# Two-layer decoder on one core: the experts' down product as three fp32r products, its weights split ahead of the loop

## What is computed

```python
xn = _layernorm(x, ln_gamma, ln_beta); xf = xn.reshape(-1, D)
logits = jnp.clip(xf @ router_w.T, -CLAMP, CLAMP)
probs = jnp.clip(softmax(logits), ROUTER_EPS, 1.0)
topk_p, topk_i = jax.lax.top_k(probs, 2)
dense_gate = zeros(N, 8).at[tokens, topk_i].add(topk_p)
for eid in range(8):
    xe = xf * dense_gate[:, eid:eid + 1]
    gate, up = jnp.split(xe @ gate_up_w[eid].T, 2, axis=-1)
    hidden = jax.nn.silu(gate) * up
    out = out + hidden @ down_w[eid].T
return x + out
```

## Time and profile before

| what | value |
|---|---|
| median of 3 runs | 1375.52 us (1372.28 to 1378.48) |
| the profiled execution's own time | 1373.03 us |
| its span | 1371.3 us |
| TensorE busy (PE) | 1188.6 us, 87% |
| VectorE (DVE) | 863.6 us, 63% |
| ScalarE (ACT) | 763.2 us, 56% |
| GpSimd (POOL) | 584.4 us, 43% |
| mean granted clock of TensorE | 0.939 |
| L2388 down matmuls, x312 records | 73.9 us, 380 ns mean |
| L2567 low parts of weights, x78 | 92.1 us, 1222 ns mean |
| L2427 high parts of weights, x78 | 77.9 us, 1047 ns mean |
| L2296 scatters, x39 | 86.2 us, 2211 ns mean |

### The profile page before, as it was taken

One profiled execution on the slowest core, in us unless ns is written; L12 is line 12 of the kernel. 1 busy time (PEld: TensorE's weight loads), 2 busy tenths in 40 slices (PEclk: granted clock), 3 DMA queues, 4 the chain that ended last, 5 costly groups with the idle time before them and its releaser, 6 DMA issues. The chain is left out here.

```text
span 1371.3 us, 24976 instructions
## 1 busy us (share of the span) xinstructions
PE 1188.6 (87%) x8059; PEld 867.2 (63%) x8060; DVE 863.6 (63%) x1528; ACT 763.2 (56%) x2082; POOL 584.4 (43%) x616
## 2 busy tenths in 40 slices
PE   7888589566999999999999999999898439999992
PEld 4544367445666767677666777766676337777781
DVE  2588799874345555665355555675687766777773
ACT  2598457434556565565555655664365245565653
POOL 1155447656436332321563321200267405666663
PEclk9999779888799999999999999999999658999996
DMA  9100000001010010000100000100720232322325
GB/s 302 40 1 1 0 1 2 1 16 31 17 32 16 16 32 17 1 16 17 32 16 17 16 17 6 43 1 1 287 83 1 74 126 40 50 50 47 52 42 138
DMA packets 42136, 58.27 MB, mean 42 GB/s; under 512 B 6608, under 2 KB 34640, under 8 KB 42032
## 3 DMA queue, kind: packets, MB, share of 16 engines
q1 hardware_dynamic: 34544, 46.70, 11.3%
q0 software_dynamic: 7488, 10.23, 4.6%
HBM read 32.80 MB, written 13.63 MB: 34 GB/s over the span
## 5 line engine op out<-in xcount | busy, mean ns | idle before, releaser
L2017 DVE TENSOR_REDUCE ga_neg_top<-ps 128x1 f32<-128x128 f32 (+7 forms) x256 | 182.1, 753 | 194.4 <-PE ps L1787 194.0
L1898 ACT ACTIVATE ga_e<-ps,ga_neg_top 128x128 f32<-128x128 f32 (+7 forms) x256 | 188.4, 744 | 7.6 <-DVE ga_neg_top L2017 6.8
L1907 ACT COPY ga_e_tr<-ps 128x512 f32<-128x512 f32 (+3 forms) x192 | 92.2, 480 | 174.4 <-PE ps L1796 171.7
L1796 PE MATMUL ps<-ident,ga_e 128*128 128x128 f32 x1152 | 165.1, 279 | 0.8 <-DVE ga_e_tr L2025 0.8
L1812 PE MATMUL ps<-ga_e_tr,ga_v 128*64 128x256 f32 x1152 | 151.7, 391 | 4.1 <-ACT ga_att L1915 4.1
L1796 PEld LDWEIGHTS ps<-ident,ga_e 128*128 128x128 f32 x1152 | 123.3, 142 | 28.0 <-ACT ga_e L1898 14.7
L2025 DVE COPY ga_e_tr<-ps 128x128 f32<-128x128 f32 (+3 forms) x192 | 106.0, 552 | 35.1 <-PE ps L1796 34.7
L2567 DVE TENSOR_TENSOR ex_w_lo<-ex_gate_up,ex_w_hi 128x1024 fp32r<-128x1024 f32 x78 | 92.1, 1222 | 31.3 <-ACT ex_w_hi L2427 30.8
L1972 POOL TENSOR_TENSOR ga_q_lo<-shared,ga_q_hi 128x1024 fp32r<-128x1024 f32 x15 | 35.6, 2371 | 175.4 <-ACT ga_q_hi L1888 175.4
L1812 PEld LDWEIGHTS ps<-ga_e_tr,ga_v 128*64 128x64 f32 x1152 | 72.4, 136 | 49.0 <-issue 23.4
L2296 POOL DMA_INDIRECT summed_rows<-shared,ex_tile_target x39 | 86.2, 2211 | 38.0 <-DMA summed_rows<-shared,ex_tile_target 21.0
(11 more groups left out here) (330 smaller groups left out, 2696.7 us busy)
## 6 DMA issues: line engine op xcount, KB each, us to landing
shared<-shared SPq DMA_DIRECT2D x80, 128.0 KB, 2.4
ex_gate_up<-in_ex_gate_up SPq DMA_DIRECT2D x1, 8192.0 KB, 24.4
ex_down<-in_ex_down SPq DMA_DIRECT2D x1, 4096.0 KB, 35.7
x_tr<-in_x_tr SPq DMA_DIRECT2D x4, 512.0 KB, 6.7
x_nat<-in_x SPq DMA_DIRECT2D x1, 2048.0 KB, 11.8
gated_rows<-shared SPq DMA_DIRECT2D x8, 256.0 KB, 2.2
gated_rows<-x_tr SPq DMA_DIRECT2D x8, 256.0 KB, 2.3
x_tr<-summed_rows SPq DMA_DIRECT2D x8, 256.0 KB, 5.0
```

The source lines that it names most:

```text
L1796: last = nc.tensor.transpose(ps_tr[n % 2][:, (kb - k0) * P:(kb - k0 + 1) * P], e[half][t % 2][:, kb * P:(kb + 1) * P], core.ident[:])
L1898: nc.scalar.activation(e[half][t % 2][:, 0:blocks(t) * P], ps_scores(t, half), ACT.Exp, bias=neg_top[t % 2][:, half:half + 1], accum_out=s ...
L1907: nc.scalar.copy(e_tr[g % 2][:, k0:k1, half, t % 2 * P:(t % 2 + 1) * P], ps_tr[n % 2][:, 0:(k1 - k0) * P].rearrange("p (k t) -> p k t", t= ...
L2017: nc.vector.tensor_reduce(neg_top[t % 2][:, half:half + 1], ps_scores(t, half), AX.X, ALU.max, negate=True).then_inc(top_ready, 1)
```

## The change

The down product becomes three fp32r products of four matmuls each: hidden high x down high, hidden high x down low, hidden low x down high. The tile of transposed hidden is split by ScalarE (high) and VectorE (low) where VectorE copied it before. The down weights are split once for each expert, outside the slots: high by ScalarE, into the place of x_nat and x_tr, low by VectorE, in place of the fp32 weights. ScalarE does four experts among its router copies and four behind the written gated rows; VectorE does four behind its last scaling and two each in the first two steps of the loop. ScalarE's and VectorE's loops get one lag more: a step does the second half of the gate and up weights of its tile, and at its end the first half of the next tile's, and the split of hidden now opens the step. TensorE's order stays.

```diff
+        down_hi = core.x_rounded[:].rearrange("p (e k n) -> p e k n", e=EXPERTS, k=KF)
+        down_lo = weights.down_rounded[:]
+        KEPT = EXPERTS // 2
+        hidden_hi, hidden_lo = (core.shared_rounded[:, start:start + FF].rearrange("p (k t) -> p k t", k=KF)
+                                for start in (D + 2 * FF, 5 * D + 3 * FF))
+        def split_low(dve, x, ready):
+            dve.wait_ge(down_hi_ready, x + 1)
+            nc.vector.tensor_tensor(expert_columns(down_lo, x), weights.down[:, x].rearrange("p k n -> p (k n)"),
+                                    expert_columns(down_hi, x).bitcast(F32), ALU.subtract).then_inc(ready, 1)
...
 (TensorE, end of a step)
-                        pe.wait_ge(hidden_tr_copied, u2 + 1)
+                        if at(u2, 0):
+                            pe.wait_ge(down_first_ready, KEPT)
+                            pe.wait_ge(down_lo_ready, EXPERTS - KEPT)
+                        pe.wait_ge(hidden_lo_ready, u2 + 1)
                         need(pe, down_copied, u2)
-                        for k in range(KF):
-                            last = nc.tensor.matmul(core.ps_y[:, 0:D], hidden_tr[:, k, :],
-                                                    weights.down[:, bass.ds(y, 1), k, :].rearrange("p a n -> p (a n)"),
-                                                    start=(k == 0), stop=(k == KF - 1))
+                        for i, (values, w) in enumerate(((hidden_hi, down_hi), (hidden_hi, down_lo), (hidden_lo, down_hi))):
+                            columns = expert_columns(w, y)
+                            for k in range(KF):
+                                last = nc.tensor.matmul(core.ps_y[:, 0:D], values[:, k, :], columns[:, k, :],
+                                                        start=(i == 0 and k == 0), stop=(i == 2 and k == KF - 1))
...
 (ScalarE, ahead of the loop)
+                act.wait_ge(weights.loaded, 16 * weights.LOADS)
+                act.wait_ge(doubled_ready, TILES // DOUBLED)
                 for n in range(TILES // BATCHED):
...
+                    x, rest = divmod(n + 1, TILES // BATCHED // KEPT)
+                    if rest == 0:
+                        act.wait_ge(scaled_ready, x * GROUPS_OF_TILES // KEPT)
+                        split_high(x - 1)
...
+                act.wait_ge(gated_written, 16 * 2 * GROUPS_OF_TILES)
+                for x in range(KEPT, EXPERTS):
+                    split_high(x)
                 act.wait_ge(sources_ready, 1)
...
 (ScalarE, a step)
+                def step(ahead, t, u1, u2, turn):
+                    if u2 is not None:
+                        act.wait_ge(hidden_tr_ready, u2 + 1)
+                        need(act, down_ready, u2)
+                        nc.scalar.copy(hidden_hi[:], core.ps_c.rearrange("p (k t) -> p k t", k=KF)).then_inc(hidden_hi_ready, 1)
                     if t is not None:
+                        weights_high(t, 1, (turn - 1) % 2)
...
+                    if ahead is not None:
+                        weights_high(ahead, 0, turn % 2)
                     if u2 is not None:
                         act.wait_ge(down_ready, u2 + 1)
...
 (VectorE, behind the scaling)
+                for x in range(KEPT):
+                    split_low(dve, x, down_first_ready)
...
 (VectorE, a step)
+                def step(ahead, t, u1, u2, turn):
                     if u2 is not None:
+                        dve.wait_ge(hidden_hi_ready, u2 + 1)
+                        nc.vector.tensor_tensor(hidden_lo[:], core.ps_c.rearrange("p (k t) -> p k t", k=KF), hidden_hi[:].bitcast(F32),
+                                                ALU.subtract).then_inc(hidden_lo_ready, 1)
                     if t is not None:
+                        weights_low(t, 1, (turn - 1) % 2)
...
+                    if ahead is not None:
+                        weights_low(ahead, 0, turn % 2)
+                    if at(t, 0) or at(t, 1):
+                        first = KEPT + t * (EXPERTS - KEPT) // 2
+                        for x in range(first, first + (EXPERTS - KEPT) // 2):
+                            split_low(dve, x, down_lo_ready)
...
+                lagged(dve, SLOT_TILES, 3, step, turns=True)
```

More of the change, by code:

```diff
@@ L118, in __init__ @@
         self.sem_ctx, self.stage_sems = ctx, []
+        with ExitStack() as same_place:
+            self.x_rounded = self.sb(same_place, "x_rounded", [P, 2 * TILES * D], F32R)
         self.x_nat = self.sb(ctx, "x_nat", [P, TILES, D])
@@ L123, in __init__ @@
         self.wide_weights = self.sb(ctx, "wide_weights", [P, KD, NQ * HD])
+        with ExitStack() as same_place:
+            self.shared_rounded = self.sb(same_place, "shared_rounded", [P, 4 * SEQ], F32R)
         self.shared = self.sb(ctx, "shared", [P, 4 * SEQ])
@@ L2077, in __init__ @@
         self.gate_up = core.sb(ctx, "ex_gate_up", [P, EXPERTS, KD, 2 * FF])
+        with ExitStack() as same_place:
+            self.down_rounded = core.sb(same_place, "ex_down_rounded", [P, EXPERTS, KF, D], F32R)
         self.down = core.sb(ctx, "ex_down", [P, EXPERTS, KF, D])
@@ L2362, in step @@
                         pe.wait_ge(hidden_ready, u2 + 1)
-                        need(pe, hidden_tr_copied, u2)
+                        need(pe, hidden_lo_ready, u2)
                         for k in range(KF):
@@ L2401, in _, with split_high @@
                                          scale=2.0).then_inc(doubled_ready, 1)
+                def split_high(x):
+                    nc.scalar.copy(expert_columns(down_hi, x), weights.down[:, x].rearrange("p k n -> p (k n)")).then_inc(down_hi_ready, 1)
+                act.wait_ge(weights.loaded, 16 * weights.LOADS)
+                act.wait_ge(doubled_ready, TILES // DOUBLED)
                 for n in range(TILES // BATCHED):
@@ L2415, in _, with weights_high @@
                             last.then_inc(gated_ready, 1)
+                act.wait_ge(gated_written, 16 * 2 * GROUPS_OF_TILES)
+                for x in range(KEPT, EXPERTS):
+                    split_high(x)
                 act.wait_ge(sources_ready, 1)
-                act.wait_ge(gated_written, 16 * 2 * GROUPS_OF_TILES)
                 act.wait_ge(summed_written, 16 * (TILES // DOUBLED + 1))
                 act.wait_ge(weights.loaded, 16 * weights.LOADS)
-                def step(t, u1, u2, turn):
-                    if t is not None:
[L2424 to L2428, removed]
+                def weights_high(t, k, buffer):
+                    x = expert_at(act, t)
+                    need(act, gate_up_ready, t - 1)
+                    nc.scalar.copy(w_hi[buffer][:, k, :], weights.gate_up[:, bass.ds(x, 1), k, :]
+                                   .rearrange("p a n -> p (a n)")).then_inc(w_hi_ready, 1)
+                def step(ahead, t, u1, u2, turn):
[3 more added lines that the diff above has]
+                        nc.scalar.copy(hidden_hi[:], core.ps_c.rearrange("p (k t) -> p k t", k=KF)).then_inc(hidden_hi_ready, 1)
+                    if t is not None:
+                        weights_high(t, 1, (turn - 1) % 2)
                     if u1 is not None:
@@ L2554, in _, with weights_low @@
                 dve.wait_ge(weights.loaded, 16 * weights.LOADS)
[L2556 removed]
+                def weights_low(t, k, buffer):
+                    x = expert_at(dve, t)
+                    dve.wait_ge(w_hi_ready, KD * t + k + 1)
+                    need(dve, gate_up_ready, t - 1)
+                    nc.vector.tensor_tensor(w_lo[buffer][:, k, :], weights.gate_up[:, bass.ds(x, 1), k, :].rearrange("p a n -> p (a n)"),
+                                            w_hi[buffer][:, k, :].bitcast(F32), ALU.subtract).then_inc(w_lo_ready, 1)
+                def step(ahead, t, u1, u2, turn):
                     if u2 is not None:
[L2558 to L2561 removed]
+                        dve.wait_ge(hidden_hi_ready, u2 + 1)
+                        nc.vector.tensor_tensor(hidden_lo[:], core.ps_c.rearrange("p (k t) -> p k t", k=KF), hidden_hi[:].bitcast(F32),
+                                                ALU.subtract).then_inc(hidden_lo_ready, 1)
                     if t is not None:
[L2563 to L2568 removed]
+                        weights_low(t, 1, (turn - 1) % 2)
                     if u1 is not None:
```

20 lines of the change are left out of this document (6 added, 14 removed).

## The result

The changed kernel takes 1380.21 us (median of 10 runs, 1379.47 to 1382.61), the kernel before 1376.08 beside it: ratio 1.0031, 95% interval [1.002, 1.0041], 4.1 us (0.3%) slower.

A forecast was written before the change was run, and what follows sets the result against it. It took a ring of TensorE, ScalarE and VectorE, 10.66 us for two slots, as the bound. Front +0.3, start +1.8, slots -5.1 and end -0.5 gave -3.5 us: 1372.0, range 1362 to 1383.

The forecast's parts named there:

- likeliest case: Expert loop: 5.18 us a slot, period 5.05 to 5.30, total changed by -8 to +1 us; chance 0.50.
- TensorE's sequencer: Steady loop: its register operations ahead of the next transposes set the slot, two slots in 10.10 us, 5.18 with the branch.
- TensorE's own work: One slot: 3.49 us plus twelve down matmuls at 0.118, 1.42, so TensorE alone needs 4.91 us.
- The arc over ScalarE and VectorE: Steady loop: weights split ahead, hidden product done 4.70 us into the next slot, under TensorE's 4.91, so not the bound.
- can follow 5.18: Steady loop: GpSimd's unhindered cycle of 4.64 us fits the forecast slot of 5.18 unless two subtractions hold it twice.
- Rival B: Loop: GpSimd becomes the bound, held by both subtractions; cycle 5.54 us, +7.1, giving 1385 us; chance 0.15.
- Start of the loop: First slots: VectorE's four down splits there delay the third slot and what follows, +1.8 us.
- TensorE's ring: Loop start: waits among TensorE, ScalarE and VectorE, by which a slot starts at 1157.15 against 1155.39.
- other causes: Anywhere: effects of either sign, a colder clock in the longer first waits among them; chance 0.04.
- Ahead of the loop: Before the loop: one VectorE subtraction goes ahead of GpSimd's last addition, +0.3 us; +2.7 if three go.
- End: Last scatters, chained by their landings: the first lands 0.7 us earlier with no subtraction beside it, counted as -0.5.
- Rival A: Loop: TensorE becomes the bound at 4.91 us a slot, about -10 us, giving 1365 us; chance 0.27.

The follow-up runs named there:

- e11: Changed kernel with the small copies on VectorE and every down product taken from expert 0 at a fixed address: 1360.2 us, 0.9883 of the kernel before.
- e5: Changed kernel with the small copies of the rows' numbers moved from GpSimd to VectorE: 1364.6 us, 0.9908 of the kernel before.
- e7: Changed kernel with VectorE's low-part subtractions cut to 16 of 1024 columns in the hardware loop: 1363.6 us, 0.9903 of the kernel before.
- e6: Changed kernel with VectorE's last four down splits one in each of slots 1 to 4: 1378.4 us, 1.001 of the kernel before.
- e2: Kernel before with only the gate and up weights split half a slot ahead, down product still fp32: 1376.7 us, 0.9993 of the kernel before.

## Why the prediction was wrong

Forecast -3.5, measured +4.1: 1380.2 lies inside the range of 1362 to 1383, but on the other side of no change. It lies there by luck, and so does the slot: 5.27 is inside the 5.05 to 5.30 of my likeliest case, but GpSimd sets it and not what I named.

- **TensorE's sequencer** is the step that failed, and the likeliest case stood on it: "twelve register operations". There are eight, since the two uses of the high parts share their addresses (four FUSED_REGOPS and four ALU_OP in the rows under e11). The start I had right: low part ready at T + 7.69, which is some 2.5 into the next slot; in e5 the first register operation starts 2.56 into it (1205.01 - 1202.45). With 8 x 0.13 + 0.85 two slots need T + 9.58, under 2 x 4.91: no bound. Slots of 4.85 in the changed kernel (slots 4 to 10) and of 4.83 in e11, which has no such operations, show it. Only the branch's part was real, 0.05 a slot.
- **TensorE's own work** was right: 1.42 for twelve, 4.91 a slot; measured 0.1175 apart and 4.85. **The arc over ScalarE and VectorE** was right too: it let TensorE run at 4.85 wherever GpSimd did (slots 4 to 10 of the changed kernel, e5, e11).
- **GpSimd** "can follow 5.18, as long as the two subtractions, now apart, don't hold it twice": they do. Rival B had the mechanism: the holding is spread over the copies. The rule of the Trainium skill ("SBUF — State Buffer", "Who interferes with whom") agrees with the 0.04 above and with e7. But its price was wrong: with 0.9 of holding I had 5.54, the runs show 0.56 and 5.25, a little less than the 0.67 before. By the cycle alone B would have been a gain.
- **Start of the loop**, +1.8, is the term that turned the sign: +7.2 by the scatters. I followed TensorE's ring there and not GpSimd's cycle. The ring was sized well: step 2 to 3 is 7.27 and 7.33 in e7 and e5, where I had 7.5; in the changed kernel it is 8.15, half of the difference by the lower clock, which I had only among the other causes, with a chance of 0.04. But GpSimd's eight cycles from the first scatter on are 1.3 longer than its free 4.68 (47.8 / 8 - 4.68): 1.2 by holding, 0.1 by the wait for TensorE; before it was 0.7. What the bunching of the splits and the lower clock do together is seen in e6 (2.2 of the 4.6 go). Of the first scatter's 2.6, the split ahead alone makes 1.9 (e2). The rest was not taken apart.
- **Ahead of the loop** +0.3: measured +0.14 from the stage's start to the first low part. **End** -0.5: -1.4 and +0.3.
- **Rival A** (TensorE the bound, 4.91) has the slot that the kernel reaches once its copies are moved: 4.89.

## What to carry to other kernels

Before an engine on the arc is made faster, work out the cycle of every engine beside it with all its small instructions; here a copy of one number per partition was on the path, since it can be held 1.0 us by another engine's subtraction. Where such an engine has hardly anything to spare (GpSimd's held cycle filled the slot of 5.33 before), move its small work first: the same change that lost 0.3% gave 0.9% with two copies moved. And compare by stage: the stages ahead, the same in all kernels, moved by up to 6.7 us between profiled executions.

## What the runs showed of the hardware

- Which GpSimd instruction is held depends on the phase and locks in: the scatter in every slot before but the last three (2.09 or more against 1.56), a copy or two in every slot of the steady part after, none in e5's steady part with the same subtractions. In the rows read, a held copy ends 0.04 after the subtraction; a scatter that starts ahead of a subtraction (1265.25, the subtraction at 1265.47) keeps its 1.59.
- A GpSimd copy of 128x1 int32 takes 0.20 behind a gather, but 0.76 behind a scatter, whose record it overlaps by 0.56. It costs more than its time: with it 0.79 pass to the next indirect DMA, without it 0.31. On VectorE the same copy takes 0.145.
- fp32r matmuls of 256 columns on the whole array start 0.1175 apart, twelve in 1.41 us, against 1.73 for four in fp32 (eight records).
- After TensorE had waited 2.05 us at the start of the changed loop, its granted clock was 0.50 for 3.3 us, and the twelve down matmuls of that slot took 2.65 instead of 1.41. After a wait of 1.7 at the same place (e5, e7) it stayed at 1.00; what decides this was not tested.
